# Layer 1's expert rows: weighted sums in the last norm, or scatter-added onto residual rows in memory

## The reference

```python
logits = jnp.einsum('bsd,de->bse', x, Wg) + bg          # x: the normed rows
topk_vals, topk_idx = jax.lax.top_k(logits, 2)
topk_w = jax.nn.softmax(topk_vals, axis=-1)
h = jax.nn.relu(jnp.einsum('bsd,edf->bsef', x, W1) + b1)
eo = jnp.einsum('bsef,efd->bsed', h, W2) + b2
mixed = jnp.sum(jnp.take_along_axis(eo, topk_idx[..., None], axis=2) * topk_w[..., None], axis=2)
y = mixed + x
return gamma * (y - mean(y)) * rsqrt(var(y) + 1e-5) + beta
```

## Time and profile before

| | |
|---|---|
| time, median of 3 runs | 1462.54 us (1461.04 to 1464.5) |
| the profiled execution, first to last instruction (its span) | 1461.2 us |
| PE busy | 1340.8 us, 92% of the span |
| ACT busy | 985.1 us, 67% |
| DVE busy | 591.4 us, 40% |
| POOL busy | 174.4 us, 12% |

### The profile page before, as it was taken

One profiled execution on the slowest core, in us unless ns is written; L12 is line 12 of the kernel. 1 busy time (PEld: TensorE's weight loads), 2 busy tenths in 40 slices (PEclk: granted clock), 3 DMA queues, 4 the chain that ended last, 5 costly groups with the idle time before them and its releaser, 6 DMA issues. The chain is left out here.

```text
span 1461.2 us, 31936 instructions
## 1 busy us (share of the span) xinstructions
PE 1340.8 (92%) x13180; PEld 707.4 (48%) x13180; DVE 591.4 (40%) x1253; ACT 985.1 (67%) x1186; POOL 174.4 (12%) x188
## 2 busy tenths in 40 slices
PE   7799999999999998999769999999999986399994
PEld 4333333333333655999633334334334325299983
DVE  7412143152332354434451123562662664544435
ACT  4599999999998233322359995995995980155532
POOL 2000000000000331233200000000000000166540
PEclk9999999999999999999979999999999996599998
DMA  7671010100100914211438010110111115022214
GB/s 209 164 124 28 20 27 21 27 20 20 27 24 21 308 58 141 79 52 45 110 109 175 20 29 13 35 28 16 34 28 48 66 35 169 18 66 73 70 59 173
DMA packets 66268, 101.88 MB, mean 70 GB/s; under 512 B 10218, under 2 KB 48366, under 8 KB 65224
## 3 DMA queue, kind: packets, MB, share of 16 engines
q1 hardware_dynamic: 60168, 83.52, 21.0%
q0 software_dynamic: 5952, 16.26, 3.4%
HBM read 69.04 MB, written 26.21 MB: 65 GB/s over the span
## 5 line engine op out<-in xcount | busy, mean ns | idle before, releaser
L1317 ACT ACTIVATE arena<-ps 128x1024 f32<-128x1024 f32 x556 | 565.5, 1306 | 52.8 <-PE ps L1057 52.8
L1057 PE MATMUL ps<-arena 99*32 99x512 bf16 x6656 | 467.7, 384 | 17.2 <-PEq L867 10.9
L1057 PEld LDWEIGHTS ps<-arena 99*32 99x32 bf16 x6656 | 148.1, 95 | 419.5 <-issue 165.5
L1317 ACT ACTIVATE wqkv<-ps 128x1024 f32<-128x1024 f32 x276 | 306.3, 1306 | 20.6 <-PE ps L1057 20.6
L1073 PE MATMUL ps<-arena 128*32 128x512 f32 x2224 | 288.7, 593 | 0.8 <-ACT arena L1317 0.8
L1413 DVE COPY work<-ps 128x512 f32<-128x512 f32 x30 | 20.7, 691 | 346.3 <-PE ps L1073 346.3
L1899 PE MATMUL ps<-work,arena 128*128 128x128 f32 x1184 | 147.7, 281 | 2.7 <-DVE work L1991 1.6
L1899 PEld LDWEIGHTS ps<-work,arena 128*128 128x128 f32 x1184 | 146.5, 197 | 7.0 <-DVE work L1991 4.0
L1073 PE MATMUL ps<-wqkv,arena 128*32 128x512 f32 x1104 | 143.5, 593 | 0.0
L991 POOL DMA_INDIRECT work<-xn_img,fetch x62 | 60.3, 972 | 585.3 <-DVEq L1037 540.7
L1913 PE MATMUL ps<-arena,work 128*128 x496 | 117.2, 380 | 0.0
(11 more groups left out here) (219 smaller groups left out, 1198.2 us busy)
## 6 DMA issues: line engine op xcount, KB each, us to landing
arena<-in_ew SPq DMA_DIRECT2D x16, 512.0 KB, 5.7
arena<-q_img SPq DMA_DIRECT2D x32, 192.0 KB
arena<-y_tok SPq DMA_DIRECT2D x12, 512.0 KB, 6.7
arena<-k_img SPq DMA_DIRECT2D x8, 624.0 KB, 13.7
q_img<-work SPq DMA_DIRECT2D x18, 256.0 KB, 2.7
k_img<-work SPq DMA_DIRECT2D x21, 208.0 KB, 2.4
arena<-q_img SPq DMA_DIRECT2D x32, 128.0 KB
arena<-in_rg SPq DMA_DIRECT2D x8, 512.0 KB, 7.8
```

The lines of the kernel that those rows point to most:

```text
L1057: last = nc.tensor.matmul(ps[i * VW:(i + 1) * VW, buf + j, :], k2[0:ROWS + SHIFT, h, at:at + VW], q2[0:ROWS + SHIFT, h, :], start=True, st ...
L1317: nc.scalar.activation(probs[(b * STEPS + u) % RING], ps[:, buf:buf + 2, :], ACT.Exp, scale=SCALE).then_inc(s_exp, 1)
```

## The change

In layer 1 alone, and in code lines of before:

- Four small DVE operations after L1596 split the 32 weights of each partition into three 16-bit parts (`wts_parts`).
- `weights` on DVE, put ahead of `places`: three products of `in_tile` with those parts, 1248 elements per partition each. PE's `row_weights`, after `lists`: 32 matrix products of `in_row` with that table, 117 columns each. DVE's `row_weights` adds the three parts: now each row of each tile has its token's weight in a column `row_weight[:, i]`.
- `sums_places` on DVE, after `places`: three small operations make `dest` point to the same row for first and second choice.
- `y_tok` of layer 1 has 2048 + 128 rows. SP stores the normed rows (the residual) there, besides the store to `xn_img` that it makes anyway: four more stores of 512 KB, three of them in the attention loop.
- `finish` gets a second DVE instruction: after the bias, the row times its weight.
- The scatter adds to the rows in memory (`compute_op=ALU.add`) where it overwrote them.
- ACT's 32 diagonals (L1973), PE's identity products (L1939) and sums (L1947) go.
- At the end SP loads four times 512 KB, not eight, and DVE and ACT work from the loaded rows.

```diff
-        y_tok = [nc.dram_tensor(f"y_tok{l.n}", [3 * S + P, D], F32).ap() for l in layers]
+        y_tok = [nc.dram_tensor(f"y_tok{l.n}", [S + P if l.mlp else 3 * S + P, D], F32).ap() for l in layers]
...
+                    def row_weights():
+                        pe.wait_ge(s_wb, 1)
+                        for i in range(T):
+                            last = nc.tensor.matmul(ps[:, 7, 0:3 * NTL], in_row[l][:, i, :], weight_in_tile[:, i, :],
+                                                    start=(i == 0), stop=(i == T - 1))
+                        last.then_inc(s_wr, 1)
...
                         lists()
+                        row_weights()
...
+                        chain(nc.vector.tensor_copy(wts_parts[:, 0, :, :], wts[:, 2:0:-1, :]))
+                        chain(nc.vector.tensor_tensor(wts_rest[:, :, :], wts[:, 2:0:-1, :], wts_parts[:, 0, :, :],
+                                                      ALU.subtract))
+                        chain(nc.vector.tensor_copy(wts_parts[:, 1, :, :], wts_rest[:, :, :]))
+                        chain(nc.vector.tensor_tensor(wts_parts[:, 2, :, :], wts_rest[:, :, :], wts_parts[:, 1, :, :],
+                                                      ALU.subtract))
...
+                    def sums_places():
+                        chain(nc.vector.tensor_scalar(code[:, 0:NTL], dest[:, 0:NTL], float(S), -float(S), ALU.is_ge,
+                                                      ALU.mult))
+                        chain(nc.vector.tensor_copy(pad[:, 0:NTL], dest[:, 0:NTL]))
+                        dve.wait_ge(s_pl, 1)
+                        chain(nc.vector.tensor_tensor(dest[:, 0:NTL], pad[:, 0:NTL], code[:, 0:NTL], ALU.add))
+                    def weights():
+                        n = NTL
+                        for i in range(3):
+                            last = nc.vector.tensor_tensor(
+                                weight_in_tile[:, :, i * n:(i + 1) * n], in_tile[l][:, :, 0:n],
+                                wts_parts[:, i, :, :].rearrange("p k t -> p (k t)").unsqueeze(2).broadcast_to([P, T, n]),
+                                ALU.mult)
+                        last.then_inc(s_wb, 1)
+                    def row_weights():
+                        n = NTL
+                        dve.wait_ge(s_wr, 1)
+                        chain(nc.vector.tensor_copy(row_weight, ps[:, 7, 0:n]))
+                        chain(nc.vector.tensor_tensor(row_weight, ps[:, 7, n:2 * n], row_weight, ALU.add))
+                        chain(nc.vector.tensor_tensor(row_weight, ps[:, 7, 2 * n:3 * n], row_weight, ALU.add))
...
                     if l == 1:
+                        weights()
                         places()
+                        sums_places()
+                        row_weights()
...
                                 store_rows(b - 1)
+                                store_rows(b - 1, y_tok[1][0:S, :], s_yb)
...
                         store_rows(NB - 1)
+                        store_rows(NB - 1, y_tok[1][0:S, :], s_yb)
+                        sp.wait_ge(s_yb, 16 * NB)
...
-                        for k in range(L.top):
-                            sp.dma_start(got[k][:, b * TB:(b + 1) * TB, :],
-                                         y_tok[l][k * S:(k + 1) * S, :].rearrange("(p t) d -> p t d", p=P)
-                                         [:, b * TB:(b + 1) * TB, :]).then_inc(s_back[b], 16)
+                        sp.dma_start(got[:, b * TB:(b + 1) * TB, :],
+                                     y_tok[l][0:S, :].rearrange("(p t) d -> p t d", p=P)
+                                     [:, b * TB:(b + 1) * TB, :]).then_inc(s_back[b], 16)
...
-                            nc.vector.tensor_tensor(rows_out[i % 2], ps[:, 6 + i % 2, 0:D],
-                                                    eb2[:, bass.ds(e, 1), :].rearrange("p a n -> p (a n)"), ALU.add
-                                                    ).then_inc(s_y, 1)
+                            chain(nc.vector.tensor_tensor(rows_out[i % 2], ps[:, 6 + i % 2, 0:D],
+                                                          eb2[:, bass.ds(e, 1), :].rearrange("p a n -> p (a n)"),
+                                                          ALU.add))
+                            nc.vector.tensor_scalar(rows_out[i % 2], rows_out[i % 2], row_weight[:, i:i + 1], None,
+                                                    ALU.mult).then_inc(s_y, 1)
...
-                                if t % 2 == 0:
-                                    dve.wait_ge(s_acc, t // 2 + 1)
-                                last = nc.vector.bn_stats(stats[:, t - i * n, :], summed(t))
+                                if t % TB == 0:
+                                    dve.wait_ge(s_back[t // TB], 16)
+                                last = nc.vector.bn_stats(stats[:, t - i * n, :], got[:, t, :])
...
-                            in_=rows_out[i % 2], in_offset=None).then_inc(s_st[i % 2], 16)
+                            in_=rows_out[i % 2], in_offset=None, compute_op=ALU.add if l else ALU.bypass
+                            ).then_inc(s_st[i % 2], 16)
```

More of the change, by code:

```diff
@@ L222, in build @@
             in_row[L.n], at = view(work, at, [L.slots, P], BF16)
-        diag = view(arena, 14 * G, [2, NT, P])[0]
-        got = [view(arena, i * PROBS, [NT, D])[0] for i in range(2)]
+        weight_in_tile, at = view(arena, 14 * G, [layers[1].slots, 3 * layers[1].tiles], BF16)
+        row_weight, at = view(arena, at, [layers[1].tiles])
+        wts_parts, at = view(arena, at, [3, 2, NT], BF16)
+        wts_rest, at = view(arena, at, [2, NT])
+        got = view(arena, 0, [NT, D])[0]
         flat = lambda t: t.rearrange("p a b -> p (a b)")
@@ L981, in layer @@
             s_gb, s_xb = only(l, "norm_params_scaled"), only(l, "x_with_beta")
-            s_dg, s_acc = only(l, "weights_on_diagonals"), only(l, "rows_summed")
+            s_wb, s_wr, s_yb = only(l, "weights_in_tiles"), only(l, "weights_in_rows"), only(l, "rows_with_bias")
             s_sc, s_nr = only(l, "norm_scales"), only(l, "rows_normed")
@@ L1763, in _, with store_rows @@
                         load_k2(sp, l, g, s_k2[g])
-                    def store_rows(b):
-                        sp.dma_start(xn_img[l].rearrange("(p t) d -> p t d", p=P)[:, b * TB:(b + 1) * TB, :],
-                                     xn[:, b * TB:(b + 1) * TB, :]).then_inc(s_img, 16)
+                    def store_rows(b, to=xn_img[l], done=s_img):
+                        sp.dma_start(to.rearrange("(p t) d -> p t d", p=P)[:, b * TB:(b + 1) * TB, :],
+                                     xn[:, b * TB:(b + 1) * TB, :]).then_inc(done, 16)
                     for b in range(NB):
@@ L1843, in _ @@
                         fetch_rows(pool, i)
-            summed = lambda t: ps[:, t // 2, t % 2 * D:(t % 2 + 1) * D]
             with nc.Block() as block:
@@ L1934, in _ @@
                         preps[1][3](pe)
[L1935 to L1950, removed]
                 @block.scalar
@@ L1970, in _ @@
                             copy_gate(act, i + 2)
[L1971 to L1974, removed]
                     if l == 0:
@@ L1982, in _ @@
                             act.wait_ge(s_sc, t // (2 * TB) + 1)
-                            nc.scalar.activation(got[0][:, t, :], summed(t), ACT.Identity,
+                            nc.scalar.activation(got[:, t, :], got[:, t, :], ACT.Identity,
                                                  bias=scales[:, 1, t:t + 1], scale=scales[:, 0, t:t + 1]
@@ L2054, in _ @@
                                     out=x[:, ts, :].rearrange("p t d -> p (t d)"),
-                                    in0=got[0][:, ts, :].rearrange("p t d -> p (t d)"), scalar=tg,
+                                    in0=got[:, ts, :].rearrange("p t d -> p (t d)"), scalar=tg,
                                     in1=x[:, ts, :].rearrange("p t d -> p (t d)"), op0=ALU.mult, op1=ALU.add)
@@ L2074, in _ @@
                             dve.wait_ge(s_nr, (b + 1) * TB)
-                            chain(nc.vector.tensor_tensor(got[0][:, ts, :], got[0][:, ts, :],
+                            chain(nc.vector.tensor_tensor(got[:, ts, :], got[:, ts, :],
                                                           gamma.unsqueeze(1).broadcast_to([P, TB, D]), ALU.mult))
                             dve.wait_ge(s_xb, NT)
-                            nc.vector.tensor_tensor(x[:, ts, :], x[:, ts, :], got[0][:, ts, :], ALU.add
+                            nc.vector.tensor_tensor(x[:, ts, :], x[:, ts, :], got[:, ts, :], ALU.add
                                                     ).then_inc(s_xf, 1)
```

## The result

The changed kernel takes 1497.88 us (median of 4 runs, 1496.99 to 1498.78); the kernel before, run beside it, 1461.79 (1459.44 to 1464.50). The ratio is 1.0242, 95% interval 1.0221 to 1.0263: slower by 36 us. The forecast was slower by 13, with a range up to 1501. Mechanism and sign were right; one term of the sum, the time that a scatter needs more when it adds, was too small.

The account below looks back on a forecast made before the run. The prediction took PE, at 3.73 us per tile in layer 1's expert loop, as the bound before, and waiting scatters after. Transfer-bound, 39 d - 18.25 with d = 0.8 gave +12.95, a median of 1475.5 us; range 1459 to 1501.

Parts of the forecast that it names:

- the term d: Expert loop of layer 1: what an adding scatter needs above a plain one, from start to landing; taken as 0.8 us.
- the upper end: High end of d, 1.8 us: rows first fetched as a gather does (2.8 less POOL's 1), then added and written.
- Its last paragraph: Signs: scatter landing 3.2, tiles every 4.0; wrong if landing is under 2.8 or POOL's own instruction, not the landing, grows.
- Transfer-bound: Whole-span sum if each scatter's wait for the landing before binds the expert loop: 39 d - 18.25, +12.95 at d = 0.8.
- Routing: Before the expert loop: DVE's three `weights` products ahead of `places` make POOL's first gather later by 3.3 us.
- Hand-over: Expert loop: DVE's added scaling per tile makes each scatter start 0.41 us later, which counts once.
- PE's rows: Expert loop: four row buffers feed PE while POOL's scatter waits, so the wait reaches PE only through `rows_out`.
- The end: Layer 1's end, first load to DVE's last instruction: 26.03 us where it was 33.09, shorter by 7.06, modelled on layer 0.
- PE-bound sum: Whole-span sum if PE's 3.73 us per tile stays the bound: +3.3 + 0.41 + 2 d - 7.06 = -3.35 + 2 d.
- The second read is free: Rival on the adding scatter: d under 0.22, PE stays the bound, 1459.2 to 1459.6 us, faster; chance 0.18.
- the scatter fills its margin only: Rival on the adding scatter: d from 0.22 to 0.54, -2.9 to +2.8 us, no change; chance 0.16.
- The memory read goes ahead of the write: Rival on the adding scatter: d over 1.45, up to 1.8, +52 us, 1514.5; chance 0.14.

Follow-up runs that it names:

- plain version: The changed kernel with layer 1's scatter overwriting rows where it added to them, all else kept: 1458.56 us, ratio 0.9974 to the kernel before.
- two sums: The changed kernel with tiles adding in turn to two tensors, each scatter waiting for the one two tiles back, DVE adding both at the end: 1466.29 us.

## Why the prediction was right in direction and short in size

- **The step that failed: the term d, taken as 0.8.** It was summed from 0.41 (a second read on the engines) and 0.4 (memory answers later than on-chip rows), "since the addition does both things". Measured: 1.4. The flight alone did grow by the 0.8 of that sum, but that agreement is luck: by the packets the engines were busy for 0.78 us longer per scatter (18.2 us on 16 engines for 5.8, in the median), not 0.41, and the 0.4 of a later answer stands nowhere as a delay of its own, neither ahead of the first packet nor behind the last. What was missing is 0.6 of POOL's own instruction. The prediction held POOL's part fixed without saying why: it even subtracted it from the gather's landing, as the 1 us of POOL's part, to get the upper end. It priced transfer and memory from rows, but not the engine that prepares the transfer, although the instruction's 0.99 was on the table as the first part of every landing. Its last paragraph names the case, POOL's own instruction growing, as one in which it would be wrong; it should have been in the sum, or at least on top of the upper end.
- **What one tenth was worth.** Transfer-bound, the sum is 39 d - 18.25. With d = 1.4 it gives +36.35; the medians differ by 36.1. So the miss of 22.4 us is 39 times 0.6, 23.4, to within 1 us. That it fits so closely is in part luck. Against the 35.5 between the two spans the sum at d = 1.4 is 0.85 too high. From first to last scatter it is 2.1 too low (+38.3 for +40.43), since five landings were late in place of three; but the profiled execution happened to reach the reciprocal 2.39 earlier, which no term is about, and the end was 0.35 shorter than forecast.
- **Routing, 3.3 (ends 1.2 and 3.3): 3.21.** The three products took 4.18, 4.13 were forecast, and the nearest row by kind of operation was the right one. PE's 32 products (3.33) and DVE's small operations were hidden, as costed: they end at 1263.84, and PE's first transposes of gathered rows start at 1268.04.
- **Hand-over, 0.41: 0.42.**
- **PE's rows.** The prediction let the wait reach PE "only through `rows_out`", with four row buffers in between. The profile also puts 12 of PE's waits in the loop (7.4 us) down to the landing of a gather, which stands behind the waiting scatter on POOL. PE was off the path there, so the sum doesn't change.
- **The end, 26.03: 25.68.** Layer 0's end was a good model for layer 1's.
- **PE-bound sum, -3.35 + 2 d.** The plain version tests it at d = 0: -3.0 by the medians.
- **The rivals.** "The second read is free" and "the scatter fills its margin only" fall with 1.4 against 0.54. "The memory read goes ahead of the write" (1.45 to 1.8) was nearest in time, but not in kind: at half the bytes 0.3 us of the flight's share go, and the first packet starts as soon after POOL's row as a plain scatter's, so it isn't one delay put in front.
- **The rule weighed in the prediction.** The Trainium skill (Collectives: The Full Stack, section "The bandwidth ceiling: the fold count and why AG ≠ RS ≠ AR") says that the addition costs nothing itself and a second read halves the rate; by that alone d would be 0.41. Measured was 1.4, and the measurement decides: for this scatter of 128 KB the stretch of its packets is 2.6 times as long (1.32 for 0.51), and 0.6 are POOL's. Another page fits better: the Trainium skill (Perfetto Trace Analysis, section "DMA Instruction — SWDGE (GPSIMD)") says that the profile's interval of such an instruction ends when the last descriptor is written, not when the data has moved. The trace agrees: 1.59 us with whole rows and with half their columns, while the landing went from 3.8 to 3.3.

## What to carry to other kernels

Read the landing of a transfer in two parts, what the issuing engine takes to prepare it and the flight, and price both anew when the kind of transfer changes. Where transfers that update the same memory must follow one another, compare landing plus hand-over with the bound engine's time per tile: here 3.20 against 3.73 was a margin of 0.53, and what exceeds it counts once per tile. Two sums in place of one break such a chain, but they must be paid for at the end.

## What the runs showed that I had not expected

- POOL's instruction for an adding scatter of 128 rows takes 1.59 us in place of 0.99, and 1.45 in place of 0.91 for 64 rows: mostly a fixed price.
- An adding scatter sends 96 packets more than a plain one of the same 128 rows (9696 against 5952 in the whole run), one for each row, and its packets keep the 16 engines busy for 1.14 us in place of 0.36.
- POOL's vector work beside it gets slower: the beta addition took 1.31 in the mean, 0.74 before, and begins 1.05 us after the scatter's start, while that row still runs.
- Some scatters land late: adding ones up to 5.7 us where each waits for the one before, at most 4.2 with two sums, 3.4 with half the columns, 3.3 with half the rows; plain ones too, up to 3.9 in the kernel before. In each of the five late ones of the changed kernel a packet of 16 KB of the queue `instruction` runs during the flight and takes 0.9 to 1.5 us, and the last one to eight of the scatter's packets start only as it ends. Here is the first of the five, from start to landing:

```profile
q0 software_dynamic: 221, 0.32, 35.4%
q8 instruction: 1, 0.02, 1.9%
```

Four other scatters have such a packet in the time to their landing, but ahead of their own packets or when these were nearly or wholly done. With half the rows none coincides with a scatter's packets, with half the columns three touch their start or their end. So the lower maxima there may be chance. No run moves these packets, so this is what the traces show together, not a tested cause.
